# A slot table of 64-byte lines, and gathers that leave out the rows of empty slots, in an attention and mixture-of-experts kernel

## The chip, the cores and the metric

One core of one Trainium2 chip. The time is device microseconds of one launch. The kernel before was timed three times: 1839.61, 1846.12 and 1847.39 us, median 1846.12. The profile is of one execution, whose span from the first to the last instruction is 1837.7 us.

## The reference

The input `x` is 16 sequences of 1024 tokens of 512 values, float32. In short:

```
x = x + cross_attention(layernorm(x), context)      # 8 heads of 64, 64 context rows a sequence
X = layernorm(x)                                    # 16384 tokens, 512 values
scores = sigmoid(X @ gate.T)                        # 32 experts
idx    = top_k(scores + bias, 4)                    # 4 experts a token; the bias only selects
w      = scores[idx] / sum(scores[idx])
pos    = how many earlier (token, choice) pairs took the same expert
valid  = pos < 512                                  # an expert takes its first 512 pairs, no more
ye     = (silu(xe @ W1) * (xe @ W3)) @ W2           # per expert, on its 512 rows xe
out    = x + sum over choices of w * ye[expert, pos], where valid
           + silu(X @ sw1.T) * (X @ sw3.T) @ sw2.T  # shared expert, for all tokens
```

How the tokens spread over the experts depends on the drawn bias and weights. Worked out from the reference on its own inputs: of 65,536 (token, choice) pairs 6900 are valid. Thirteen experts have all 512 slots taken (1, 2, 5, 10, 14, 16, 17, 19, 20, 21, 23, 24, 28), four have 26, 87, 128 and 3 (11, 15, 22, 27), the other fifteen have none.

## The kernel before

The work has two phases. The **token phase** takes the 16384 tokens in 128 tiles of 128, in a software pipeline written out by hand: step `n` does, for tile `n - lag`, each stage with its lag (the constants `X_LOAD` = 2 to `TABLE` = 20). PE computes the attention scores (L417), the mix of values (L432, from probabilities that are turned by a DMA transpose into `pt_h` and `pt_l`), the routing logits and the shared expert (L459, L469). For a group of four tiles DVE then picks the four best experts of each token, counts with PE's help how many earlier tokens took the same expert, and writes into `slot` the number `expert * 512 + pos`, or a number past the end of the table where `pos` is over 511 (`slot_list`, L997). The normalized tokens and, in the last 32 columns, their 32 expert weights (`wfull`) are stored as rows of 544 floats in `x2aug`; the rows 16384 to 16895 of it are zero.

At the start SP stores zeros in those rows and fills the table (L347) with the numbers of the zero rows, so that an empty slot names one of them. This `fill` is made by POOL's iota and stands in `xr`, the ring of token tiles, before tokens are loaded there.

The **expert phase** takes the experts 0 to 31 in order, in a second hand-written pipeline (`GATHER`, `TURN`, `UP`, `DOWN`, `SCATTER` = 0, 1, 2, 3, 5 steps behind). SP loads the whole table into `idx` in two DMAs (L1229 and L1230), the first for experts 0 and 1. POOL gathers the expert's 512 rows in four chunks of 128 (L1245) into a ring of six buffers `rows`, PE transposes them (L1306) and multiplies (L1280, L1320), DVE scales the result by the weight that came with the row (L1426), and POOL adds it into `out` with an indirect, accumulating store (L1257). A round of four such stores waits until the round before has landed (`added`), since two experts may add to one row. Rows of empty slots are added to 512 rows behind the output proper. In POOL's queue the order of a step is the scatter of expert n - 5, then the gather of expert n.

A chunk's gather from the seventh expert on waits for `y_read` of the expert that used the buffer before.

Of the kernel before, what the change touches and what calls it, by code (L numbers as in the profile page):

```python
# [30 lines left out]
P = 128  # L31
# [12 lines left out]
ROW = D + E  # L44
PAD = CAP
EPS = 1e-5
SKIP = float(1 << 20)
# [70 lines left out]
def after(eng, sem, count):  # L118

    if count > 0:  # L120
        eng.wait_ge(sem, count)

def build(nc, x, xT, ctxT, wqT, wk, wv, wo, bo, gateT, bias, w1, w3, w2, sw1T, sw3T, sw2T, out):
    x2aug = nc.dram_tensor("x2aug", (TOKENS + PAD, ROW), F32, kind="Internal").ap()
    table = nc.dram_tensor("slot_table", (SLOTS, 1), I32, kind="Internal").ap()
    tokens_and_experts(nc, x, xT, ctxT, wqT, wk, wv, wo, bo, gateT, bias, w1, w3, w2, sw1T, sw3T, sw2T, out, x2aug, table)

def tokens_and_experts(nc, x, xT, ctxT, wqT, wk, wv, wo, bo, gateT, bias, w1, w3, w2, sw1T, sw3T, sw2T, out, x2aug, table):  # L130
    stack = ExitStack()
    with stack:
# [83 lines left out]
        ht_l = sb("ht_l", [P, KI, 4 * P], F32R)  # L216
        tok = sb("tok", [P, TILES], I32)
        slot = sb("slot", [P, 2, 4, TOP], I32)
        slot_f = sb("slot_f", [P, 4, 8], F32)
# [16 lines left out]
        zrow = xr[:, 8:10, :].rearrange("p a d -> p (a d)")[:, 0:ROW]  # L236
        fill = xr[:, 10, 0:SLOTS // P].bitcast(I32)
        down_raw = xr[:, 11, :].bitcast(BF16).rearrange("p (c d) -> p c d", c=KI)
# [63 lines left out]
        with nc.Block() as block:  # L302
            @block.sync
            def _(sp):
# [20 lines left out]
                def set_up():  # L325
# [17 lines left out]
                    for r in range(TOKENS, TOKENS + PAD, P):  # L343
                        sp.dma_start(x2aug[r:r + P, :], zrow).then_inc(fill_stored, 16)
                        sp.dma_start(out[r:r + P, :], zrow[:, 0:D]).then_inc(fill_stored, 16)
                    sp.wait_ge(fill_set, 1)
                    sp.dma_start(table.rearrange("(e p c) o -> p e (c o)", e=E, p=P),  # L347
                                 fill.rearrange("p (e c) -> p e c", e=E)).then_inc(fill_stored, 16)
# [48 lines left out]
                for n in range(STEPS):  # L397
                    step(n)
                for r in range(2):
                    sp.wait_ge(scattered[r], GROUPS // 2 * 256)  # L400
# [341 lines left out]
            def _(pool):  # L742
                def file(t, first, end):
                    if t is None:
                        return
                    g, i = t // 4, t % 4
                    if i == 0 and first == 0:
                        if g == 0:
                            pool.wait_ge(fill_stored, (2 * PAD // P + 1) * 16)
                            pool.wait_ge(const_set, 11)  # L750
                        pool.wait_ge(slots_ready, g + 1)
                        pool.sem_inc(passed, 1)
                    for q in range(first, end):
                        pool.indirect_dma_start(  # L754
                            table, bass.IndirectOffsetOnAxis(ap=slot[:, g % 2, i, q:q + 1], axis=0),
                            tok[:, t:t + 1], None, bounds_check=SLOTS - 1, oob_is_err=False).then_inc(scattered[g % 2], 16)

                def step(n):
# [17 lines left out]
                    if t is not None:  # L776
# [11 lines left out]

                pool.iota(fill.rearrange("p (e c) -> p e c", e=E), [[0, E], [1, CAP // P]], base=TOKENS,
                          channel_multiplier=CAP // P).then_inc(fill_set, 1)  # L790
# [31 lines left out]
            def _(dve):  # L822
# [164 lines left out]
                def slot_spread(g):  # L987
                    dve.wait_ge(placed, g + 1)
                    after(dve, slots_ready, g)
                    dve.sem_inc(passed, 1)  # L990
# [3 lines left out]
                def slot_list(g):  # L994
                    dve.wait_ge(spread, g * 4 + 4)
                    after(dve, scattered[g % 2], (g // 2) * 256)
                    dve.tensor_scalar(slot[:, g % 2, :, :], slot_f[:, :, 0:TOP], -1.0, TOPSLOT, ALU.mult,  # L997
                                      ALU.add).then_inc(slots_ready, 1)
# [162 lines left out]
def experts(nc, stack, ident, w1, w3, w2, out, x2aug, table):  # L1161
# [11 lines left out]
    ident_r = sb("ident_r", [P, P], F32R)  # L1173
    idx = sb("idx", [P, E, CHUNKS], I32)
    down_w = sb("down_w", [P, 2, KI, D], F32R)
    weights_rest = sb("weights_rest", [P, 3072 - 256 - 2048], F32)
    up_more = sb("up_more", [P, WEIGHT_SETS - EARLY_SETS, KD, 2 * I], BF16)
# [8 lines left out]
    he_l = sb("he_l", [P, 2, KI, CAP], F32R)  # L1186
    ye = sb("ye", [P, 4, CHUNKS, D], F32)

    TE_ps = [pb(f"TE_ps{n}") for n in range(2)]
# [17 lines left out]
    down_src = w2.rearrange("e (c p) d -> e p c d", p=P)  # L1207
    table_src = table.rearrange("(e p c) o -> p e (c o)", e=E, p=P)

# [18 lines left out]
    def experts_sync(sp):  # L1228
        sp.dma_start(idx[:, 0:2, :], table_src[:, 0:2, :]).then_inc(idx_first, 16)  # L1229
        sp.dma_start(idx[:, 2:E, :], table_src[:, 2:E, :]).then_inc(idx_loaded, 16)  # L1230
        for e in range(WEIGHT_SETS, E):
            load_weights(sp, e)

    def experts_gpsimd(pool):
        def gather(e):
# [7 lines left out]
            for c in range(CHUNKS):  # L1243
                landed = gathered[r] if e else first_rows[c]
                pool.indirect_dma_start(  # L1245
                    rows[:, r, c, :].bitcast(F32), None, x2aug,
                    bass.IndirectOffsetOnAxis(ap=idx[:, e, c:c + 1], axis=0),
                    bounds_check=TOKENS + PAD - 1, oob_is_err=False).then_inc(landed, 16)

        def scatter(e):  # L1250
# [3 lines left out]
            for c in range(CHUNKS):  # L1254
                pool.wait_ge(y_read, e * CHUNKS + c + 1)
                pool.sem_inc(passed, 1)
                pool.indirect_dma_start(  # L1257
                    out, bass.IndirectOffsetOnAxis(ap=idx[:, e, c:c + 1], axis=0),
                    ye[:, e % 4, c, :], None, bounds_check=TOKENS + PAD - 1, oob_is_err=True,
# [236 lines left out]
```

## Time and profile before

| | busy us | share of the span |
|---|---|---|
| span of the profiled execution | 1837.7 | |
| PE (matmul) | 1666.3 | 91% |
| DVE | 1384.2 | 75% |
| ACT | 1075.6 | 59% |
| POOL | 1257.2 | 68% |
| DMA queue q1 (SP's) | | 56.2% of 16 engines |
| DMA queue q0 (POOL's) | | 20.7% of 16 engines |

The profile does not list a total of its own beside the span; the three timed runs are those above. The token phase reaches to about 1358 us on PE, the expert phase from about 1385 us to the end. Busy time of an engine says how long its instructions ran, not that they were needed by the end; what stands in brackets behind a row of the timeline is how long the engine had been idle before it and what released it. "DMA share" is the mean busy share of the 16 DMA engines; it can come out over 1.

### The profile page before, as it was taken

The page shows a single profiled execution, that of the slowest core. Times are in us where ns is not written, and L with a number is a line of the kernel's source. Part 1 is how long each engine was busy: PE and PEld are TensorE (multiplying, and loading weights), DVE is VectorE, ACT ScalarE, POOL GpSimd, SP SyncE. Part 2 cuts the span into 40 slices and gives each one's busy share as a digit, 9 for nine tenths or more (in the row PEclk, how much of TensorE's full clock was granted, in tenths as well). Part 3 has the DMA queues.
Part 4 walks back from the last instruction along what each step waited for, and adds up shares of the span by engine and source line. Part 5 has one row for each costly group of instructions (what it writes and reads, how often), then busy time and mean ns, then how long its engine had stood idle before and what let it go on. Part 6 is the DMA issues. An engine that isn't in the chain of part 4 may idle for free. (4 is left out here: it accounts for less than half of the span.)

```text
span 1837.7 us, 31673 instructions
## 1 busy us (share of the span) xinstructions
PE 1666.3 (91%) x8928; PEld 1041.6 (57%) x8928; DVE 1384.2 (75%) x3450; ACT 1075.6 (59%) x2376; POOL 1257.2 (68%) x1109
## 2 busy tenths in 40 slices
PE   6896789999999999999999999999736999999993
PEld 4563455656656666666666666665423555555551
DVE  4765667888899889789879888999734777777772
ACT  4773556667777767777777767776403444444440
POOL 1333556677777777777777777777775787888774
PEclk8998899999999999999999999999877999999996
DMA  9549997787678667666756766666677999999985
GB/s 220 142 128 97 132 117 167 147 167 159 154 183 177 155 162 167 164 173 167 176 152 162 185 167 157 168 169 165 153 192 170 217 230 222 233 224 212 172 140 73
DMA packets 474482, 308.61 MB, mean 168 GB/s; under 512 B 339138, under 2 KB 381378, under 8 KB 474308
## 3 DMA queue, kind: packets, MB, share of 16 engines
q1 hardware_dynamic: 429252, 237.07, 56.2%
q0 software_dynamic: 45056, 69.52, 20.7%
q8 instruction: 73, 1.20, 0.3%
q14 instruction: 101, 0.83, 0.2%
HBM read 134.07 MB, written 105.25 MB: 130 GB/s over the span
## 5 line engine op out<-in xcount | busy, mean ns | idle before, releaser
L754 POOL DMA_INDIRECT slot_table<-tok,slot x512 | 538.0, 1051 | 140.9 <-issue 136.8
L763 POOL TENSOR_TENSOR xt_l<-xt,xt_h 128x512 fp32r<-128x512 f32 x128 | 165.4, 1292 | 191.5 <-ACT xt_h L639 191.5
L1257 POOL DMA_INDIRECT out<-ye,idx x128 | 202.9, 1585 | 70.7 <-issue 36.6
L432 PE MATMUL O_ps<-m_h,pt_h 128*128 128x512 f16 x512 | 200.2, 391 | 52.5 <-DMA pt_l<-p_l 52.0
L687 ACT ACTIVATE prob<-S_ps,rs 128x512 f32<-128x512 f32 x128 | 88.0, 687 | 244.1 <-DVE S_ps L1047 218.7
L417 PE MATMUL S_ps<-a_h,xt_h 128*128 128x512 f32 x512 | 222.4, 434 | 5.6 <-POOL xt_l L763 5.0
L778 POOL TENSOR_TENSOR prob<-prob,rsum 128x512 f32<-128x512 f32 x128 | 135.8, 1061 | 115.8 <-DVE rsum L1083 115.4
L417 PE MATMUL S_ps<-a_h,xt_l 128*128 128x512 f32 x512 | 201.3, 393 | 0.0
L417 PE MATMUL S_ps<-a_l,xt_h 128*128 128x512 f32 x512 | 201.1, 393 | 0.0
L432 PE MATMUL O_ps<-m_l,pt_h 128*128 128x512 f16 x512 | 199.1, 389 | 0.0
L432 PE MATMUL O_ps<-m_h,pt_l 128*128 128x512 f16 x512 | 198.8, 388 | 0.0
L1245 POOL DMA_INDIRECT rows<-x2aug,idx x128 | 132.8, 1037 | 43.0 <-issue 41.2
L432 PEld LDWEIGHTS O_ps<-m_h,pt_h 128*128 128x128 f16 x512 | 50.6, 99 | 138.0 <-DMA pt_l<-p_l 60.4
L1034 DVE TENSOR_TENSOR x_l<-x,x_h 128x512 f16<-128x512 f32 x128 | 91.6, 716 | 49.0 <-ACT x_h L664 48.9
L1372 ACT ACTIVATE xe_h<-TE_ps 128x512 f16<-128x512 f32 x128 | 75.7, 592 | 72.9 <-PE TE_ps L1306 72.9
L1418 DVE TENSOR_TENSOR xe_l<-TE_ps,xe_h 128x512 f16<-128x512 f32 x128 | 87.8, 687 | 40.2 <-ACT xe_h L1372 38.2
L417 PEld LDWEIGHTS S_ps<-a_h,xt_h 128*128 128x128 f32 x512 | 97.4, 190 | 35.6 <-issue 16.9
L1306 PE MATMUL TE_ps<-ident_r,rows 128*128 128x128 f32 x512 | 67.4, 257 | 49.9 <-DMA rows<-x2aug,idx 29.4
L1320 PE MATMUL YE_ps<-down_w,he_h 128*128 128x512 f32 x256 | 110.9, 433 | 0.6 <-DVE he_l L1412 0.6
L417 PEld LDWEIGHTS S_ps<-a_l,xt_h 128*128 128x128 f32 x512 | 97.2, 190 | 24.1 <-issue 7.4
L1354 ACT ACTIVATE the<-GE_ps 128x512 f32<-128x512 f32 x64 | 38.2, 597 | 121.8 <-PE GE_ps L1280 121.8
L417 PEld LDWEIGHTS S_ps<-a_h,xt_l 128*128 128x128 f32 x512 | 96.6, 189 | 21.4
(199 smaller groups left out, 4679.0 us busy)
## 6 DMA issues: line engine op xcount, KB each, us to landing
xt<-in_xT SPq DMA_DIRECT2D x128, 256.0 KB, 3.3
xr<-in_x SPq DMA_DIRECT2D x64, 512.0 KB, 4.3
x2aug<-x SPq DMA_DIRECT2D x128, 256.0 KB
out<-xr SPq DMA_DIRECT2D x64, 512.0 KB, 3.5
up_more<-in_w SPq DMA_DIRECT2D x36, 256.0 KB, 5.3
slot_table<-tok,slot POOLq DMA_INDIRECT x512
up_w<-in_w SPq DMA_DIRECT2D x28, 256.0 KB, 4.8
down_more<-in_w SPq DMA_DIRECT2D x18, 256.0 KB, 6.3
```

What stands on the lines that cost most here:

```text
L417: last = pe.matmul(S_ps[t % 2][:, :], left[:, kc, :], right[:, b % 2, kc, :], start=(m == 0), stop=(m == 3 * KD - 1))
L432: last = pe.matmul(O_ps[:, :], left[:, t % 2, p, :], right[:, b % 2, p, :], start=(m == 0), stop=(m == 3 * PAIRS - 1))
L687: act.activation(prob[:, t % 2, :, :], S_ps[t % 2][:, :].rearrange("p (h j) -> p h j", h=H), ACT.Exp, scale=rs[:, q % 2, 0, t % 2:t % 2 + ...
L754: pool.indirect_dma_start(table, bass.IndirectOffsetOnAxis(ap=slot[:, g % 2, i, q:q + 1], axis=0), tok[:, t:t + 1], None, bounds_check=SLO ...
L763: pool.tensor_tensor(xt_l[:, t % 2, :, :], xt[:, t % 2, :, :], xt_h[:, t % 2, :, :].bitcast(F32), ALU.subtract).then_inc(xt_lo, 1)
L778: pool.tensor_tensor(prob[:, t % 2, :, :], prob[:, t % 2, :, :], rsum[:, :].unsqueeze(2).to_broadcast([P, H, SKV]), ALU.mult).then_inc(pro ...
L1034: dve.tensor_tensor(x2_l[:, :], x2[:, s13 % 2, :], x2_h[:, :], ALU.subtract).then_inc(x2_lo, 1)
L1245: pool.indirect_dma_start(rows[:, r, c, :].bitcast(F32), None, x2aug, bass.IndirectOffsetOnAxis(ap=idx[:, e, c:c + 1], axis=0), bounds_che ...
L1257: pool.indirect_dma_start(out, bass.IndirectOffsetOnAxis(ap=idx[:, e, c:c + 1], axis=0), ye[:, e % 4, c, :], None, bounds_check=TOKENS + P ...
L1320: last = pe.matmul(YE_ps[i % 2][:, :], part[:, e % 2, c, i * P:(i + 1) * P], down_w[:, e % 2, c, :], start=(n == 0), stop=(n == 2 * KI - 1))
L1372: act.activation(xe_h[:, e % TURNED, :, i * P:(i + 1) * P], TE_ps[i % 2][:, :].rearrange("p (c t) -> p c t", c=KD), ACT.Copy).then_inc(t_h ...
L1418: dve.tensor_tensor(xe_l[dst], TE_ps[i % 2][:, :].rearrange("p (c t) -> p c t", c=KD), xe_h[dst], ALU.subtract).then_inc(t_lo, 1)
```

## The change

The table's slots become lines of 16 int32 (64 bytes): the fill, the filing and the index load move lines in place of single numbers, and DVE copies the token number 16 times (`tok_line`). POOL's filing waits for that copy too. SP waits for the last stores of weights ahead of the index load. From the seventh expert on (`e >= RING`, 6) the bound of the gather ends before the zero rows, so that rows of empty slots are left out and the buffer keeps what it had there; the results computed from them go, as before, to the rows behind the output. `idx` moves to the end of the expert phase's memory.

```diff
@@ -43,6 +43,7 @@
 KI = I // P
 ROW = D + E
 PAD = CAP
+LINE = 16
 EPS = 1e-5
 SKIP = float(1 << 20)
 TOPSLOT = float(1 << 22)
@@ -123,7 +124,7 @@
 
 def build(nc, x, xT, ctxT, wqT, wk, wv, wo, bo, gateT, bias, w1, w3, w2, sw1T, sw3T, sw2T, out):
     x2aug = nc.dram_tensor("x2aug", (TOKENS + PAD, ROW), F32, kind="Internal").ap()
-    table = nc.dram_tensor("slot_table", (SLOTS, 1), I32, kind="Internal").ap()
+    table = nc.dram_tensor("slot_table", (SLOTS, LINE), I32, kind="Internal").ap()
     tokens_and_experts(nc, x, xT, ctxT, wqT, wk, wv, wo, bo, gateT, bias, w1, w3, w2, sw1T, sw3T, sw2T, out, x2aug, table)
 
 
@@ -215,6 +216,7 @@
         ht_h = sb("ht_h", [P, KI, 4 * P], F32R)
         ht_l = sb("ht_l", [P, KI, 4 * P], F32R)
         tok = sb("tok", [P, TILES], I32)
+        tok_line = sb("tok_line", [P, 2, 4, LINE], I32)
         slot = sb("slot", [P, 2, 4, TOP], I32)
         slot_f = sb("slot_f", [P, 4, 8], F32)
         wfull = sb("wfull", [P, 2, 4, E], F32)
@@ -234,7 +236,7 @@
         down_ready = sem("token_down_ready")
 
         zrow = xr[:, 8:10, :].rearrange("p a d -> p (a d)")[:, 0:ROW]
-        fill = xr[:, 10, 0:SLOTS // P].bitcast(I32)
+        fill = xr[:, 16:20, :].rearrange("p a d -> p (a d)")[:, 0:SLOTS // P * LINE].bitcast(I32)
         down_raw = xr[:, 11, :].bitcast(BF16).rearrange("p (c d) -> p c d", c=KI)
         bo_raw = xr[0:33, 12, :]
         mean_q = xr[:, 13, 0:PAIRS]
@@ -344,7 +346,7 @@
                         sp.dma_start(x2aug[r:r + P, :], zrow).then_inc(fill_stored, 16)
                         sp.dma_start(out[r:r + P, :], zrow[:, 0:D]).then_inc(fill_stored, 16)
                     sp.wait_ge(fill_set, 1)
-                    sp.dma_start(table.rearrange("(e p c) o -> p e (c o)", e=E, p=P),
+                    sp.dma_start(table.rearrange("(e p c) l -> p e (c l)", e=E, p=P),
                                  fill.rearrange("p (e c) -> p e c", e=E)).then_inc(fill_stored, 16)
 
                 def step(n):
@@ -397,6 +399,8 @@
                 for n in range(STEPS):
                     step(n)
                 for r in range(2):
+                    sp.wait_ge(w_stored[r], GROUPS // 2 * 16)
+                for r in range(2):
                     sp.wait_ge(scattered[r], GROUPS // 2 * 256)
                 experts_sync(sp)
 
@@ -748,12 +752,12 @@
                         if g == 0:
                             pool.wait_ge(fill_stored, (2 * PAD // P + 1) * 16)
                             pool.wait_ge(const_set, 11)
-                        pool.wait_ge(slots_ready, g + 1)
+                        pool.wait_ge(slots_ready, 2 * g + 2)
                         pool.sem_inc(passed, 1)
                     for q in range(first, end):
                         pool.indirect_dma_start(
                             table, bass.IndirectOffsetOnAxis(ap=slot[:, g % 2, i, q:q + 1], axis=0),
-                            tok[:, t:t + 1], None, bounds_check=SLOTS - 1, oob_is_err=False).then_inc(scattered[g % 2], 16)
+                            tok_line[:, g % 2, i, :], None, bounds_check=SLOTS - 1, oob_is_err=False).then_inc(scattered[g % 2], 16)
 
                 def step(n):
                     t = at(n, XT_SPLIT)
@@ -786,7 +790,7 @@
                 pool.affine_select(out=ident[:, :], in_=ident[:, :], compare_op=ALU.not_equal, fill=1.0,
                                    base=0, pattern=[[-1, P]], channel_multiplier=1).then_inc(ident_set, 1)
 
-                pool.iota(fill.rearrange("p (e c) -> p e c", e=E), [[0, E], [1, CAP // P]], base=TOKENS,
+                pool.iota(fill.rearrange("p (e c l) -> p e c l", e=E, l=LINE), [[0, E], [1, CAP // P], [0, LINE]], base=TOKENS,
                           channel_multiplier=CAP // P).then_inc(fill_set, 1)
                 pool.memset(earlier[:, :], 0.0).then_inc(const_set, 1)
                 pool.wait_ge(const_set, 1)
@@ -986,7 +990,7 @@
 
                 def slot_spread(g):
                     dve.wait_ge(placed, g + 1)
-                    after(dve, slots_ready, g)
+                    after(dve, slots_ready, 2 * g)
                     dve.sem_inc(passed, 1)
                     for i in range(4):
                         dve.max(slot_f[:, i, :], over[:, i, :]).then_inc(spread, 1)
@@ -994,6 +998,7 @@
                 def slot_list(g):
                     dve.wait_ge(spread, g * 4 + 4)
                     after(dve, scattered[g % 2], (g // 2) * 256)
+                    dve.tensor_copy(tok_line[:, g % 2], tok[:, 4 * g:4 * g + 4].unsqueeze(2).to_broadcast([P, 4, LINE])).then_inc(slots_ready, 1)
                     dve.tensor_scalar(slot[:, g % 2, :, :], slot_f[:, :, 0:TOP], -1.0, TOPSLOT, ALU.mult,
                                       ALU.add).then_inc(slots_ready, 1)
 
@@ -1171,9 +1176,8 @@
     up_w = sb("up_w", [P, 4, KD, 2 * I], BF16)
     down_raw = sb("down_raw", [P, 4, KI, D], BF16)
     ident_r = sb("ident_r", [P, P], F32R)
-    idx = sb("idx", [P, E, CHUNKS], I32)
     down_w = sb("down_w", [P, 2, KI, D], F32R)
-    weights_rest = sb("weights_rest", [P, 3072 - 256 - 2048], F32)
+    weights_rest = sb("weights_rest", [P, 3072 - 128 - 2048], F32)
     up_more = sb("up_more", [P, WEIGHT_SETS - EARLY_SETS, KD, 2 * I], BF16)
     down_more = sb("down_more", [P, WEIGHT_SETS - EARLY_SETS, KI, D], BF16)
     rows = sb("rows", [P, RING, CHUNKS, ROW], F32R)
@@ -1185,6 +1189,7 @@
     he_h = sb("he_h", [P, 2, KI, CAP], F32R)
     he_l = sb("he_l", [P, 2, KI, CAP], F32R)
     ye = sb("ye", [P, 4, CHUNKS, D], F32)
+    idx = sb("idx", [P, E, CHUNKS, LINE], I32)
 
     TE_ps = [pb(f"TE_ps{n}") for n in range(2)]
     GE_ps = [pb(f"GE_ps{n}") for n in range(KI)]
@@ -1205,7 +1210,7 @@
 
     up_src = [w.rearrange("e (c p) i -> e p c i", p=P) for w in (w1, w3)]
     down_src = w2.rearrange("e (c p) d -> e p c d", p=P)
-    table_src = table.rearrange("(e p c) o -> p e (c o)", e=E, p=P)
+    table_src = table.rearrange("(e p c) l -> p e c l", e=E, p=P)
 
     def up_set(e):
         r = e % WEIGHT_SETS
@@ -1226,8 +1231,8 @@
         sp.dma_start(down_set(e), down_src[e]).then_inc(set_loaded[r], 16)
 
     def experts_sync(sp):
-        sp.dma_start(idx[:, 0:2, :], table_src[:, 0:2, :]).then_inc(idx_first, 16)
-        sp.dma_start(idx[:, 2:E, :], table_src[:, 2:E, :]).then_inc(idx_loaded, 16)
+        sp.dma_start(idx[:, 0:2, :, :], table_src[:, 0:2, :, :]).then_inc(idx_first, 16)
+        sp.dma_start(idx[:, 2:E, :, :], table_src[:, 2:E, :, :]).then_inc(idx_loaded, 16)
         for e in range(WEIGHT_SETS, E):
             load_weights(sp, e)
 
@@ -1244,8 +1249,9 @@
                 landed = gathered[r] if e else first_rows[c]
                 pool.indirect_dma_start(
                     rows[:, r, c, :].bitcast(F32), None, x2aug,
-                    bass.IndirectOffsetOnAxis(ap=idx[:, e, c:c + 1], axis=0),
-                    bounds_check=TOKENS + PAD - 1, oob_is_err=False).then_inc(landed, 16)
+                    bass.IndirectOffsetOnAxis(ap=idx[:, e, c, 0:1], axis=0),
+                    bounds_check=(TOKENS if e >= RING else TOKENS + PAD) - 1,
+                    oob_is_err=False).then_inc(landed, 16)
 
         def scatter(e):
             if e:
@@ -1255,7 +1261,7 @@
                 pool.wait_ge(y_read, e * CHUNKS + c + 1)
                 pool.sem_inc(passed, 1)
                 pool.indirect_dma_start(
-                    out, bass.IndirectOffsetOnAxis(ap=idx[:, e, c:c + 1], axis=0),
+                    out, bass.IndirectOffsetOnAxis(ap=idx[:, e, c, 0:1], axis=0),
                     ye[:, e % 4, c, :], None, bounds_check=TOKENS + PAD - 1, oob_is_err=True,
                     compute_op=ALU.add).then_inc(added, 16)
```

## Rows read from the trace of the kernel before

**Rows 1.** Stretches: window, length, busy time by engine, clock, DMA share, GB/s.
```profile
100.00:136.00 36.00, 35.02 (x212) 23.53 (x211) 28.32 (x79) 26.00 (x62) 10.81 (x10) 1.00 0.55 140
...
136.00:276.00 140.00, 104.76 (x510) 61.11 (x508) 85.53 (x243) 69.60 (x163) 70.04 (x66) 0.89 1.04 115
...
276.00:420.00 144.00, 138.50 (x761) 87.53 (x761) 117.82 (x319) 98.89 (x229) 101.45 (x93) 0.99 0.79 156
...
730.00:886.00 156.00, 156.00 (x867) 99.26 (x866) 134.78 (x373) 112.23 (x262) 116.50 (x105) 1.00 0.67 168
```

**Rows 2.** Waits, 136 to 276 us: total, times, longest.
```profile
PE O_ps L432 <- DMA pt_l<-p_l: 33.8, 8, 12.7
```

**Rows 3.** DMA issues, 137 to 277 us: count, size, median to landing.
```profile
xt<-in_xT SPq DMA_DIRECT2D x10, 256.0 KB, 7.4
...
x2aug<-wfull SPq DMA_DIRECT2D x3, 64.0 KB, 7.4
```

**Rows 4.** DMA issues, 800 to 940 us.
```profile
xt<-in_xT SPq DMA_DIRECT2D x14, 256.0 KB, 3.5
...
x2aug<-wfull SPq DMA_DIRECT2D x3, 64.0 KB, 3.2
```

**Rows 5.** POOL over time: start, duration; first filings of tiles, two others.
```profile
137.14 1.17 POOL L754 DMA_INDIRECT slot_table<-tok,slot  x1 [0.17 <-issue]
...
139.93 0.98 POOL L754 DMA_INDIRECT slot_table<-tok,slot  x1 [0.30 <-issue]
...
276.63 1.00 POOL L754 DMA_INDIRECT slot_table<-tok,slot  x1 [0.16 <-issue]
...
419.78 1.00 POOL L754 DMA_INDIRECT slot_table<-tok,slot  x1 [0.17 <-issue]
...
731.26 1.00 POOL L754 DMA_INDIRECT slot_table<-tok,slot  x1 [0.17 <-issue]
...
1040.95 1.00 POOL L754 DMA_INDIRECT slot_table<-tok,slot  x1 [0.17 <-issue]
...
1375.90 0.98 POOL L754 DMA_INDIRECT slot_table<-tok,slot  x1 [0.30 <-issue]
```

**Rows 6.** The start: landing of the fill, then POOL and ACT over time.
```profile
slot_table<-xr SPq DMA_DIRECT2D x1, 64.0 KB, 13.8
...
3.71 0.48 POOL L789 IOTA xr<- 128x128 int32 x1
...
38.68 0.63 ACT L639 ACTIVATE xt_h<-xt 128x512 fp32r<-128x512 f32 x1 [6.23 <-DMA xt<-in_xT]
```

**Rows 7.** Start of the expert phase: index load and its landing, POOL, PE.
```profile
1378.49 0.46 SPq L1230 DMA_DIRECT2D idx<-slot_table  x1
...
idx<-slot_table SPq DMA_DIRECT2D x1, 60.0 KB, 4.5
...
1381.15 1.04 POOL L1245 DMA_INDIRECT rows<-x2aug,idx  x1 [4.27 <-issue]
...
1384.65 0.59 PE L1306 MATMUL TE_ps<-ident_r,rows 128*128 128x128 f32 x3 [27.19 <-DMA rows<-x2aug,idx]
```

**Rows 8.** Chain that ended last: two experts' first products.
```profile
1759.82 1.74 PE GE_ps L1280 x8
...
1772.61 1.74 PE GE_ps L1280 x8
```

**Rows 9.** POOL over time, late in the expert phase.
```profile
1744.79 1.62 POOL L1257 DMA_INDIRECT out<-ye,idx  x1 [0.53 <-issue]
...
1752.33 1.08 POOL L1245 DMA_INDIRECT rows<-x2aug,idx  x1 [0.30 <-issue]
...
1765.17 1.08 POOL L1245 DMA_INDIRECT rows<-x2aug,idx  x1 [0.30 <-issue]
...
1782.74 1.55 POOL L1257 DMA_INDIRECT out<-ye,idx  x1 [5.01 <-DMA out<-ye,idx]
```

**Rows 10.** Instructions that write `slot`: ns min/median/max.
```profile
L997 DVE TENSOR_SCALAR slot<-slot_f x32: 239/942/1299, 126.0 to 1349.0; 128x16 int32<-128x16 f32 x32
```

## The prediction

> **What bounds the kernel now.** I read busy time by stretch first, then the waits and DMA landings of the stretches that looked bad, then POOL in order of time.
>
> The token phase has two regimes. From 730 to 886 us PE is busy 156.00 of 156 us at full clock, and the DMA engines are 0.67 occupied while moving 168 GB/s. From 136 to 276 us PE is busy only 104.76 of 140 us, its granted clock is 0.89, and the DMA engines are occupied 1.04 while moving just 115 GB/s: more engine time, fewer bytes. From 276 to 420 it is nearly over (138.50 of 144 us). Just before, from 100 to 136 us, there is nothing wrong (35.02 of 36 us, DMA 0.55) [rows 1]. In the bad stretch PE's lost time is a wait for the transposed low half of the probabilities, 33.8 us in 8 waits [rows 2]. That transfer is not alone in being late: a 256 KB load of `xt` takes 7.4 us to land there and 3.5 us at 800 to 940 us, the 64 KB store of `wfull` 7.4 us against 3.2 [rows 3, 4].
>
> What begins at 137 us is the filing of tokens into the slot table [rows 5]: four indirect stores a tile, 4 bytes for each (token, choice). What fades out by 420 us is the number of those that write: a slot past an expert's 512th is out of bounds and left out. Routing worked out from the reference on its own inputs gives 512 real writes in each of tiles 0 to 4, then 442, 410, 356, 333, 275, about 112 a tile in tiles 10 to 23, 977 in all the 104 tiles after: 6900 of 65,536. So the stall follows the count of 4-byte writes, and neither the instructions (512 of them, evenly spread) nor the bytes. Consecutive tokens of one expert fill consecutive 4-byte slots, so tile 0's 512 writes lie in 37 lines of 64 bytes, some 14 writes to a line, from many DMA engines at once.
>
> In steady state a tile takes (1040.95 - 731.26) / 32 = 9.68 us. Tiles 0 to 9 took 276.63 - 137.14 = 139.5 us, against 96.8; tiles 10 to 23 took 143.2 against 135.5 [rows 5]. The excess is 42.7 + 7.7 = **50.4 us**.
>
> In the expert phase PE takes 1772.61 - 1759.82 = 12.79 us an expert [rows 8] and POOL 1765.17 - 1752.33 = 12.84 us, four adding scatters and four gathers back to back [rows 9]. POOL's chain sets the end: each round of scatters waits for the round before to land, and in the last four rounds that costs about 5 us each (5.01) with gathers long over [rows 9].
>
> **The change, part by part.** The sum is made against the profiled execution's span, 1837.7 us; the three timed runs (1839.61 to 1847.39, median 1846.12) lie 1.9 to 9.7 above, and I add 8.4, the median's.
>
> *Table writes of 64 bytes.* Each written slot now covers a line of its own and no two writes share one. The upper bound of the gain is the 50.4 us; the lower is nothing or a loss. Nearest rows: the `wfull` store is 512 pieces of 128 bytes, issued once in four tiles, and the phase stays smooth with it (3.2 us to land) [rows 4]; that speaks for full recovery. The filling of the table at the start writes 4096 pieces of 16 bytes, four to a 64-byte line, and takes 13.8 us for 64 KB [rows 6], far worse than 64 KB of `wfull`. If its extra (13.8 - 3.2 = 10.6 us for 4096) were the cost of any piece under a line's size or at it, the 5923 writes of tiles 0 to 23 would keep 15 us. I keep a third, 5 us, since the 128-byte row is the nearer in size and full in its lines. **-45 us.** PE is what is late next: in the good stretch it has no idle at all, so a tile can't go under about 9.7 us.
>
> *POOL's issues.* Same count. A store whose 128 rows were all written took 0.98 us (139.93 us) and one with none also 0.98 (1375.90) [rows 5]; the gather of 2176-byte rows at 1381.15 took 1.04 [rows 7]. At 0.02 us more each, only those behind PE's last token work count, some 20: +0.4 us, taken as **+0.5**.
>
> *DVE's copy* into `tok_line` (128x64, int32), 32 times. The nearest is `slot` at the same place: 239 ns at best, 942 median, 1299 at worst [rows 10]; 8 to 42 us of DVE in all. DVE is busy 134.78 of 156 us in steady state [rows 1], about 1.3 us free a tile, 5 a group, against 1 us of copy a group; PE hides it, at worst the copy is exposed each time (+30). I take **+1**. POOL's filing is released one DVE instruction later; behind it in POOL's queue stand the next product with `rsum` and the next split of `xt`. The copy waits for the landing of the stores of two groups back, as `slot` did.
>
> *Fill.* POOL's iota grows 16-fold. Now 0.48 us, at 3.71 us [rows 6]; even at 16 times, 7.7 us, POOL's set-up would end before 14 us, and POOL has nothing more to do until ACT has split the first `xt` tile: nothing. The store becomes 4096 pieces of 256 bytes, 1 MB. Queued behind it is the `xt` load that ACT waited 6.23 us for, until 38.68 us [rows 6]. By size, 1 MB is four `xt` loads of 3.5 us [rows 4], 14 us, no gain; at the 168 GB/s of the smooth stretch [rows 1] it is 6.2 us. It is issued some 14 us before 38.68, about 2 us of pad stores stand ahead of it, and 6.2 more put its landing near 33 us: **-4.5**, between -6 and +1.
>
> *SP's new wait* for `w_stored` stands ahead of the index load, with the later weight loads behind. The last of these stores is issued in step 145; the last filing belongs to step 147, and POOL issues it at 1375.90 with PE's token work long over [rows 5, 7]. Nothing. *Index load:* 1 MB in place of 64 KB. The second part is issued at 1378.49, and the first gather, at 1381.15, feeds PE's first transpose at 1384.65 after 27.19 us idle [rows 7]; it lands in 4.5 us now. With 1 MB it shares the engines with the first gathers. Nothing at best; at worst the 1 MB at 168 GB/s, 6.2 us, less the 2.7 between issue and gather, goes ahead of them: 3.5. **+1.** Everything after, POOL's chain too, moves with it.
>
> *Gathers that leave rows out.* Of the 13,312 rows of experts 6 to 31, 5364 are filled, so 7948 (17 MB) go. PE never waits for a gather after the first four, so the bytes buy nothing directly. POOL issues as many instructions, and by the two 0.98 us rows a left-out row is no cheaper to issue. What it frees is the scatters' landing: eight times between 1445 and 1770 us POOL waited 0.35 to 0.62 us instead of 0.30 before a round (0.53 at 1744.79 [rows 9]), 1.9 us over. **-2.** The last rounds have no gathers beside them and stay.
>
> Sum: -45 + 0.5 + 1 - 4.5 + 1 - 2 = -49; span 1789, time **1797 us**.
>
> The Trainium skill has a rule that speaks against this change ("DMA: Bandwidth & Descriptors", Specifications): transfers under 512 B make the DMA engine read, modify and write. 64 bytes are as far under as 4 are, and by it the -45 goes. The trace doesn't bear the rule out at 128 bytes, where 512 pieces land in 3.2 us; at 4 and 16 bytes it agrees. It is rival B.
>
> **The rivals.**
>
> A. Half cure: real writes of a line still stall, with the 16-byte fill's price rather than `wfull`'s. 15 to 30 us of the 50 stay: 1807 to 1822. For it: the number of real writes is unchanged, 2048 a group against 512 for `wfull`. Against: no stall with `wfull`.
>
> B. No cure: the stall is per small write, whatever its size. Then 0.5 + 1 - 4.5 + 1 - 2 = -4, 1842; without the fill's gain 1847. For it: the stall follows the count of writes. Against: `wfull` again, and that 4096 16-byte writes cost some 11 us while 5923 of 4 bytes cost 50, 8.5 ns against 2.6 a piece: the price rose with the writes to one line.
>
> C. Slower: the memory pays per line opened. Today tile 0 opens 37 lines, after the change 512. If neighbours are merged today and the 50 us are the price of lines, more lines cost more; at twice, +50, 1892. It decides against the change as soon as the line-wise price outgrows 50 + 4 us. For it: nothing directly. Against: the fill's 64 KB opens 1024 lines for 11 us, tiles 0 to 4 some 230 lines for over 20.
>
> D. The leaving out does more than I give it: POOL's issue shrinks when few rows remain. POOL runs about 10 us behind PE's results at the end, so at most 10 us more: 1787. Against: the two 0.98 us rows. That it does nothing at all costs me 2 us.
>
> **How the numbers follow.** My forecast (1785 to 1807, D's gain within it) 0.65; A 0.16; B 0.11; C 0.08. The range, 1783 to 1829, takes in the forecast and A and leaves out B and C. 0.5% is 9 us, what a measurement of this kernel can tell from no change: all of the forecast and A are faster (0.81), with 0.02 of B; the rest of B is the same (0.09); C is slower (0.08).
>
> **What would show it.** Right: from 136 to 276 us PE busy over 130 us at clock 0.98 or more and DMA occupied near 0.7; PE's wait for the transposed probabilities under 5 us there; tile 10's first filing some 40 us sooner after tile 0's; the fill landing under 10 us; the first transpose within 8 us of the last filing; POOL's round still 12.8 us and gathers still 1.04 us; the waits over 0.30 before scatters gone. Wrong: a DMA share near 1 in that stretch (A, B), a tile period over 14 us (C), or a steady tile above 9.8 us, which would be DVE's copy.

## The result: 1781.1 us, 3.4% faster

The changed kernel took 1781.11 us in the median of four runs (1776.43 to 1785.63), the kernel before, with one more run beside it, 1842.86 (1834.57 to 1847.39). The ratio is 0.9656, with a 95% interval of 0.9614 to 0.9699. In a later comparison on one chip it was 1778.98 us (six runs) against 1845.02 (seventeen), ratio 0.9645 (0.9614 to 0.9677). Forecast were 1797 us and a range from 1783: right in direction and in its main mechanism, too small in size, and the range begins 2 us too high.

The profiled execution of the changed kernel spans 1779.9 us, 57.8 less than before. Its stretch from 25 to 40 us and two of the stretches of [rows 1] (window, length, busy time of PE, PEld, DVE, ACT and POOL, clock, DMA share, GB/s):

```profile
25.00:40.00 15.00, 12.00 (x35) 6.71 (x35) 7.33 (x27) 11.59 (x32) 3.60 (x3) 0.89 0.70 194
136.00:276.00 140.00, 140.00 (x766) 87.64 (x765) 123.97 (x350) 102.54 (x242) 105.12 (x95) 1.00 0.75 176
276.00:420.00 144.00, 144.00 (x798) 92.11 (x797) 124.58 (x347) 103.11 (x242) 106.08 (x97) 1.00 0.69 168
```

The bad stretch is gone altogether. PE is busy in all 140 us where it was busy in 104.76, does 766 matmuls instead of 510, and has its full clock; the DMA engines move 176 GB/s in place of 115 with three quarters of their time. Among the waits of 136 to 276 us PE's on the turned probabilities (33.8 us, [rows 2]) no longer appears. An `xt` load is one of 15 in the same 140 us, not of 10, and `wfull` lands in 3.0 us in place of 7.4 [rows 3]:

```profile
xt<-in_xT SPq DMA_DIRECT2D x15, 256.0 KB
x2aug<-wfull SPq DMA_DIRECT2D x4, 64.0 KB, 3.0
```

POOL over time, the first filings of tiles 0, 10 and 24 and the last one of all (start, duration), against [rows 5]:

```profile
131.96 1.17 POOL L758 DMA_INDIRECT slot_table<-tok_line,slot  x1 [0.19 <-issue]
...
226.45 1.50 POOL L758 DMA_INDIRECT slot_table<-tok_line,slot  x1 [0.15 <-issue]
...
361.81 1.00 POOL L758 DMA_INDIRECT slot_table<-tok_line,slot  x1 [0.17 <-issue]
...
1314.48 0.97 POOL L758 DMA_INDIRECT slot_table<-tok_line,slot  x1 [0.30 <-issue]
```

Tiles 0 to 9 take 226.45 - 131.96 = 94.5 us where they took 139.5, tiles 10 to 23 135.4 where they took 143.2. The other lines follow from such starts. The kernel's time, stretch by stretch:

| stretch | before | after | difference | forecast |
|---|---|---|---|---|
| start to the first filing | 137.1 | 132.0 | -5.2 | -4.5 |
| tiles 0 to 9 | 139.5 | 94.5 | -45.0 | |
| tiles 10 to 23 | 143.2 | 135.4 | -7.8 | |
| tiles 24 to the last filing | 956.1 | 952.7 | -3.4 | |
| the three lines above | | | -56.2 | -43.5 |
| last filing to the first transpose | 8.8 | 9.9 | +1.2 | +1 |
| from there to the sixth expert's gather | 40.8 | 37.3 | -3.5 | 0 |
| 26 rounds of POOL | 339.7 | 344.7 | +5.0 | -2 |
| last gathers to the end | 72.5 | 73.5 | +1.0 | 0 |

Two of these lines can be followed further in the traces. Of the -3.4, 1.8 us lie in tiles 24 to 111 and most of the rest in tiles 112 to 119, a stretch that differs by up to 4.5 us between the kernels below. And the +5.0 of the 26 rounds is waiting: the time by which POOL's idle before the first adding store of a round exceeds the usual 0.30 us adds up to 8.0 us in 14 of the 26 rounds, where it was 2.5 us in 9 before. Of the five longest the profile puts three (1.0 to 1.5 us) down to the landing of the round before and two to DVE's `ye`. The longest:

```profile
1607.28 1.62 POOL L1263 DMA_INDIRECT out<-ye,idx  x1 [1.94 <-DVE ye L1432]
```

The two ends of the start and of the expert phase, to be held against [rows 6] and [rows 7]: the fill's landing, POOL's iota, ACT's second split, the index load with its landing, the first gather and the first transpose.

```profile
slot_table<-xr SPq DMA_DIRECT2D x1, 1024.0 KB, 7.5
...
3.71 2.34 POOL L793 IOTA xr<- 128x2048 int32 x1
...
33.17 0.63 ACT L643 ACTIVATE xt_h<-xt 128x512 fp32r<-128x512 f32 x1 [0.66 <-DMA xt<-in_xT]
...
1317.11 0.46 SPq L1235 DMA_DIRECT2D idx<-slot_table  x1
...
idx<-slot_table SPq DMA_DIRECT2D x1, 960.0 KB, 6.4
...
1320.04 1.04 POOL L1250 DMA_INDIRECT rows<-x2aug,idx  x1 [4.58 <-issue]
...
1324.42 1.33 PE L1312 MATMUL TE_ps<-ident_r,rows 128*128 128x128 f32 x8 [27.75 <-DMA rows<-x2aug,idx]
```

Sixteen times the bytes land in 7.5 us instead of 13.8, in as many pieces (4096, of 256 bytes instead of 16), and ACT gets the second `xt` tile 5.5 us sooner (33.17 against 38.68). While the fill was landing, the kernel before showed the same signs as while it filed tokens, a high DMA share with few bytes:

```profile
25.00:40.00 15.00, 10.21 (x21) 4.35 (x21) 4.00 (x17) 7.54 (x23) 1.88 (x2) 0.73 1.13 113
```

### The profile page after: what moved, and what is told of

Its sections match the earlier page's. It is cut to its first block and busy times, and to the rows that moved or that the text cites. A ratio compares the mean times of both kernels' runs of the same rounds, so it can differ in the third digit from the quotient of the medians.

```text
span 1779.9 us, 31706 instructions
## 1 busy us (share of the span) xinstructions
PE 1649.4 (93%) x8928; PEld 1038.4 (58%) x8928; DVE 1387.6 (78%) x3482; ACT 1074.6 (60%) x2376; POOL 1261.9 (71%) x1109
## 5 line engine op out<-in xcount | busy, mean ns | idle before, releaser
L758 POOL DMA_INDIRECT slot_table<-tok_line,slot x512 | 541.0, 1057 | 141.1 <-issue 137.2
L436 PE MATMUL O_ps<-m_h,pt_h 128*128 128x512 f16 x512 | 196.1, 383 | 8.4 <-DMA pt_l<-p_l 8.4
L436 PE MATMUL O_ps<-m_l,pt_h 128*128 128x512 f16 x512 | 194.9, 381 | 0.0
L436 PE MATMUL O_ps<-m_h,pt_l 128*128 128x512 f16 x512 | 194.8, 380 | 0.0
L1432 DVE TENSOR_SCALAR ye<-YE_ps,rows 128x512 f32<-128x512 f32 x128 | 95.2, 744 | 10.9 <-PE YE_ps L1326 8.3
```

Source lines behind the costliest of these rows:

```text
L436: last = pe.matmul(O_ps[:, :], left[:, t % 2, p, :], right[:, b % 2, p, :], start=(m == 0), stop=(m == 3 * PAIRS - 1))
L758: pool.indirect_dma_start(table, bass.IndirectOffsetOnAxis(ap=slot[:, g % 2, i, q:q + 1], axis=0), tok_line[:, g % 2, i, :], None, bounds_ ...
L1432: dve.tensor_scalar(ye[:, e % 4, i, :], YE_ps[i % 2][:, :], w, None, ALU.mult).then_inc(y_read, 1)
```

## The experiments

**Which part of the change did it.** The lines without the leaving out, the leaving out without the lines, and the change again, five rounds each on one chip. Beside them ran one more step, told further down: the adding stores leave out empty slots too.

Lines alone:
```diff
-                    bounds_check=(TOKENS if e >= RING else TOKENS + PAD) - 1,
+                    bounds_check=TOKENS + PAD - 1,
```

> The change without its gathers: every gather takes all 512 rows of its expert, the zero rows too. Theory: the 64-byte lines give the whole gain and the leaving out gives nothing, so 1781 us (1777 to 1786), the first ten tiles of the filing take 94 to 97 us, and the span's loss against the forecast sits in POOL's rounds. In the profile of the changed kernel 26 rounds of the expert phase took 339.7 - wait for wait 13.26 us a round from gather 5 to gather 31, against 13.07 before. If the leaving out is what lengthened the rounds (rival), this kernel has 13.07 again and is about 5 us faster than the changed one; if it had won the 2 us of my forecast, it is 2 us slower.

Leaving out alone (in the kernel before):
```diff
-                    bounds_check=TOKENS + PAD - 1, oob_is_err=False).then_inc(landed, 16)
+                    bounds_check=(TOKENS if e >= RING else TOKENS + PAD) - 1, oob_is_err=False).then_inc(landed, 16)
```

> The kernel before with the change's bound on the gathers from the seventh expert on, and the 4-byte table kept. Theory: the gathers are off the path, so 1843 us, within 4 us of the kernel before; tiles 0 to 9 take 139 us as before. Rival (leaving out lengthens POOL's rounds): 1848, rounds of 13.26 us. Rival (my forecast's -2): 1841, rounds of about 13.0 us with no waits over 0.30 us.

The change again, as it stands:

> The changed kernel unchanged, beside the others on the same chip. Theory: 1781 us, tiles 0 to 9 in 94.5 us. If its POOL rounds are 13.26 us again the lengthening belongs to the kernel; if they are near 13.07 it was that one execution.

The lines alone took 1785.81 us (ratio 0.9682, 0.9651 to 0.9714): 59 of the 66 us. The leaving out alone took 1839.37 against 1845.02 (0.9981, 0.9955 to 1.0008), not to be told from nothing by itself, and its bad stretch is as before: tiles 0 to 9 took 141.1 us. The change again took 1778.98, 6.8 us under the lines alone by medians, 5.3 by means with an error of about 4. Since that is more than the 2 us of my forecast I ran the lines alone again:

> 64-byte lines alone a second time, since the leaving out's share (1785.8 against 1779.0 us, single executions spread over 8 us) was larger than the 2 us of my forecast but not by more than its error. Theory: 1784 to 1787 us again, so 4 to 7 us for the leaving out. Rival: 1781 us, and the share is my 2 us.

1786.10 us (1775.75 to 1790.51), the same again. By medians the leaving out is worth 4 to 7 us. By the means of all twelve executions of the lines alone and all ten of the change (1784.0 and 1780.0, on several chips) it is 4.1 us with a 95% interval of about 3.7 to either side, so my 2 us are not excluded. Where it is saved no profile shows.

The 26 rounds of POOL took 344.7 and 343.4 us in the two profiled executions of the change and 339.6 and 337.3 in the two of the lines alone, the other way round. By the test of the expectation the lengthening would belong to the change (343.4 / 26 = 13.21 us a round). But the kernel with 4-byte writes 64 bytes apart, below, has the changed kernel's gathers and adding stores and took 336.1 us, and the four other kernels that leave out the gathers' empty rows alone took 336.1 to 337.4. So the leaving out doesn't lengthen the rounds by itself. The rounds are longer where POOL waits longer before an adding store: the excess of these waits was 8.0 and 6.9 us in the two executions of the change, 4.4 and 2.1 with the lines alone, and 0.5 to 2.1 in those five. Why it differs so between executions is open. The profiled executions of the lines alone were the second fastest and the fastest of their six (1780.9 and 1775.8 us), the change's in the later comparison its slowest (1783.2), so the profiles can't be set against each other as if they were medians.

**Size of a write, or writes that meet.** Three kernels with other tables, all with the leaving out. First: 4-byte writes, each in a 64-byte line of its own. The table stays at 1 MB, fill, index load and DVE's copy stay as in the change; the two lines that matter:

```diff
-                            tok_line[:, g % 2, i, :], None, bounds_check=SLOTS - 1, oob_is_err=False)
+                            tok[:, t:t + 1], None, bounds_check=SLOTS * LINE - 1, oob_is_err=False)
...
-                    dve.tensor_scalar(slot[:, g % 2, :, :], slot_f[:, :, 0:TOP], -1.0, TOPSLOT, ALU.mult,
+                    dve.tensor_scalar(slot[:, g % 2, :, :], slot_f[:, :, 0:TOP], -float(LINE), TOPSLOT * LINE, ALU.mult,
```

> The changed kernel, but each filing writes 4 bytes, the first word of its slot's own 64-byte line (the place is 16 times the slot). Fill and index load as in the change. Tells the size of a write from the sharing of a line. Theory (the stall is several writes meeting in one 64-byte line): tiles 0 to 9 take 94 to 98 us as in the changed kernel, 1781 us. Rival (a write of less than a line stalls, shared or not): 135 to 140 us, and some 1832 us.

It took 1775.06 us (two runs; ratio 0.9609, 0.9531 to 0.9686), and its stretch from 136 to 276 us is the changed kernel's:

```profile
136.00:276.00 140.00, 140.00 (x766) 87.61 (x765) 123.98 (x350) 102.61 (x242) 105.22 (x95) 1.00 0.74 174
```

The writes are as small and as many as in the kernel before, and nothing stalls. So it was not the size. Then lines of 16 and of 32 bytes:

```diff
-LINE = 16
+LINE = 4        # the other kernel: 8
```

> The changed kernel with lines of 4 int32: 16-byte writes, four slots to 64 bytes, and the fill in pieces of 64 bytes. Theory (sharing): the excess of tiles 0 to 9 falls with the writes to a line, by the price of the 16-byte fill 2.6 ns x 4946 writes = 10 to 15 us of the 43, tiles 0 to 9 in 104 to 112 us, 1791 to 1797 us. Rival (any write under a line): 135 to 140 us.

> The changed kernel with lines of 8 int32: 32-byte writes, two slots to 64 bytes. Theory (sharing of 64-byte lines): a small rest, tiles 0 to 9 in 96 to 103 us, 1783 to 1788 us. Rival (the unit is 32 bytes, not 64): no rest at all, 94.5 us. Rival (any write under 64 bytes): 135 to 140 us.

16 bytes took 1785.72 us, 32 bytes 1777.27 (two runs each). For 16 bytes the first filings of tiles 0 and 10 are:

```profile
132.74 1.17 POOL L758 DMA_INDIRECT slot_table<-tok_line,slot  x1 [0.19 <-issue]
...
231.38 1.50 POOL L758 DMA_INDIRECT slot_table<-tok_line,slot  x1 [0.15 <-issue]
```

and its stretch from 136 to 276 us:

```profile
136.00:276.00 140.00, 137.53 (x738) 84.59 (x738) 120.55 (x338) 98.38 (x231) 101.34 (x92) 0.99 0.79 168
```

Tiles 0 to 9: 139.5 us with sixteen slots to 64 bytes, 98.6 with four, 94.6 with two, 94.5 with one. The price falls much faster than the number of slots that share a line. What is left at four is 4.1 us there, less than the expected 10 to 15. (Tiles 0 to 9 hold 4376 real writes; the 4946 of the expectation is a slip.) This kernel also loses 4.6 us in tiles 24 to 119, but 4.5 of them in tiles 112 to 119, where few tokens are filed and where the kernel with 4-byte writes 32 bytes apart (below), which has no stall in its first ten tiles, loses 2.5 us as well. That part is not shown to be the table's.

At 32 bytes the expectation missed: 96 to 103 us for tiles 0 to 9 and 1783 to 1788 us in all if the unit that writes must not share is 64 bytes, and 94.5 us if it is 32. Measured were 94.6 us and 1777.27 us, the rival's figures. The runs so far fit a unit of 32 bytes without more, and one of 64 only if two slots to a line cost nothing.

**A small table, or a crowded line.** With 64-byte lines the table is also sixteen times as large. To tell that apart the 64 KB table was kept and its slots dealt out, neighbours 64 bytes apart (the copy on DVE is gone, fill and index load follow the new order in pieces of 256 bytes, and the gathers' empty rows are left out):

```diff
-                    dve.tensor_scalar(slot[:, g % 2, :, :], slot_f[:, :, 0:TOP], -1.0, TOPSLOT, ALU.mult, ALU.add)
+                    dve.tensor_scalar(slot_raw[:, :, :], slot_f[:, :, 0:TOP], -1.0, TOPSLOT, ALU.mult, ALU.add)
+                    dve.tensor_scalar(slot_line[:, :, :], slot_raw[:, :, :], 1023, 4, ALU.bitwise_and, ALU.logical_shift_left)
+                    dve.scalar_tensor_tensor(slot[:, g % 2, :, :], slot_raw[:, :, :], 10, slot_line[:, :, :],
+                                             ALU.logical_shift_right, ALU.bitwise_or)
```

> A 64 KB table of 4-byte slots as before, but dealt out: slot s stands at word (s mod 1024) * 16 + s / 1024, so consecutive slots lie 64 bytes apart and the 16 words of a line belong to slots 1024 apart. The leaving-out gathers are in; no lines, no DVE copy, two more small DVE operations a group, and the fill and the index load are 256 pieces of 256 bytes (64 KB each). Tells writes that meet in a line at the same time from the size or the spread of the table. Theory (meeting in a line): tiles 0 to 9 in 94 to 98 us, 1774 to 1781 us, the first transpose about 1 us sooner than with the 1 MB load. Rival (a small table is a crowded table: few banks or channels for 64 KB): 120 to 140 us for these tiles and 1810 us or more.

```profile
136.00:276.00 140.00, 140.00 (x766) 87.43 (x765) 121.42 (x351) 102.14 (x240) 104.17 (x95) 1.00 0.72 175
```

1782.67 us (0.9663, 0.9635 to 0.9692), tiles 0 to 9 in 94.5 us, with the old 4-byte writes in the old 64 KB. The rival that a small table is a crowded one has fallen too. What stalls is several writes at nearby addresses within a short time: neighbours 4 bytes apart stall, 16 bytes apart a little, 32 and 64 bytes apart not at all. Worked out from the reference's routing, one indirect store in tiles 0 to 9 puts on average 5.0 writes into each 64-byte line that it touches in the kernel before, 2.0 with slots of 16 bytes, 1.4 with 32, 1.1 in the dealt table and 1.0 with 64; the stall was 45.0, 4.1, 0.1, 0 and 0 us. In units of 32 bytes the averages are 3.2, 1.4, 1.0, 1.04 and 1.0. Both rows fit.

The time missed its 1774 to 1781 us by under 2. The first transpose came 3.6 us after the first gather; in the seven profiled executions with a 1 MB index load it came 4.4 to 5.1 us after, in the seven with a smaller one 3.5 to 3.6, so that load costs about a microsecond. Tiles 24 to 119 took 914.7 us against 910.8, spread evenly over them; the cause was not looked for.

**The end of the kernel.** The forecast's other claim was that POOL's chain sets the end, through the landing of the adding stores.

```diff
-                    ye[:, e % 4, c, :], None, bounds_check=TOKENS + PAD - 1, oob_is_err=True,
+                    ye[:, e % 4, c, :], None, bounds_check=TOKENS - 1, oob_is_err=False,
```

> The changed kernel, and the adding stores leave out empty slots as well (bound 16384 in place of 16896). 9484 of 16,384 added rows go. Theory: POOL's chain sets the end and its length hangs on the landing of each round. With experts 29, 30 and 31 empty, the wait ahead of the last rounds falls from 5.0 to 5.5 us to about 1.3 (as the table's last, empty filing shows), and the landing after the last round too: about 3 x 3.8 = 11 us; the waits within the rounds of the steady stretch go as well, some 5 to 10 us down to PE's 12.79 us an expert. In all 10 to 20 us: 1761 to 1771 us. Rival: the end hangs on PE and on the number of instructions alone, and an empty store costs a full receipt: 1779 to 1783.

1764.71 us (1762.65 to 1765.73; ratio 0.9569, 0.9539 to 0.9598), 14.3 under the change beside it. POOL at the starts of the last four rounds, and the last row of all:

```profile
1716.67 1.54 POOL L1263 DMA_INDIRECT out<-ye,idx  x1 [2.12 <-DMA out<-ye,idx]
...
1729.26 1.54 POOL L1263 DMA_INDIRECT out<-ye,idx  x1 [5.28 <-DMA out<-ye,idx]
...
1738.88 1.54 POOL L1263 DMA_INDIRECT out<-ye,idx  x1 [2.13 <-DMA out<-ye,idx]
...
1748.07 1.54 POOL L1263 DMA_INDIRECT out<-ye,idx  x1 [2.13 <-DVE ye L1432]
...
1753.61 1.54 POOL L1263 DMA_INDIRECT out<-ye,idx  x1 [0.30 <-issue]
```

After the round of expert 28, which is full, POOL waits 5.28 us; after those of 27 (three rows), 29 and 30 it waits 2.12 to 2.13, not 1.3 as expected. The excess of the waits within the 26 rounds is 1.9 us, and the rounds take 336.9 us. From the last gathers to the end it is 61.7 us instead of 73.5. Do the gathers' rows matter beside that?

```diff
-                    bounds_check=(TOKENS if e >= RING else TOKENS + PAD) - 1,
+                    bounds_check=TOKENS + PAD - 1,
...
-                    ye[:, e % 4, c, :], None, bounds_check=TOKENS + PAD - 1, oob_is_err=True,
+                    ye[:, e % 4, c, :], None, bounds_check=TOKENS - 1, oob_is_err=False,
```

> 64-byte lines, every gather takes all its rows, but the adding stores leave out empty slots. Tells how the gathers' rows cost time. Theory: they cost it only through the landing of the adding stores, which POOL waits for; with 9484 of 16,384 added rows gone those land early whatever the gathers move, so this kernel is within 2 us of the one that leaves out both (1764.7), and 26 rounds take 335 to 338 us. Rival: gathered rows cost POOL or PE time directly; then the 5 us between the lines alone and the changed kernel stay, 1770 us.

1764.92 us (0.9586, 0.9565 to 0.9607), and 26 rounds in 336.2 us: as with both left out, to the few us that two comparisons on different chips can tell. So no cost of the gathered rows' own is seen; with the empty adds gone, nothing is seen that leaving them out would win. That fits the account that they cost time by making adds land later; it doesn't show the landing itself.

**Combinations.** The dealt table with the adds left out, and 4-byte writes 32 bytes apart (`LINE = 8`, no `tok_line`) with the adds left out:

> The dealt table, and the adding stores leave out empty slots as well. If both hold: the 14 us that leaving out adds won on the 64-byte table, on top of the dealt kernel: 1758 to 1766 us. Rival: the dealt table stalls and this is over 1790.

> 4-byte writes 32 bytes apart (two slots to a 64-byte line), no copy on DVE, 512 KB of fill and index load, adds of empty slots left out too. By the 32-byte and the four-bytes-apart kernels there is no stall left: tiles 0 to 9 in 94.5 us, 1758 to 1764 us. If the DVE copy had cost anything in the changed kernel, tiles 24 to 119 fall under 910.8 us here; theory: they stay within 1 us.

1766.83 us (0.9572, 0.9544 to 0.9600) and 1764.61 (0.9562, 0.9536 to 0.9589), each under 1 us above its expected range. All versions that leave out the adds lie between 1764.6 and 1766.8 us, 12 to 17 us under the changed kernel, and no table is seen to be better than another. With 4-byte writes 32 bytes apart tiles 0 to 9 took 94.6 us, so at this distance too it isn't the size of the write that cures. Without the DVE copy tiles 24 to 119 took 913.3 us, not fewer than 910.8 and not within 1 us of it; 2.55 of the 2.6 us more lie in tiles 112 to 119. No cost of the copy is seen.

## Why the prediction was wrong in size

*The stall is due to the small writes, and lines cure it.* Right, and by more than was said; that no two writes share a line, the reason that I gave, is what counts, and their smallness is not. The step that failed is "I keep a third, 5 us": the price of the 16-byte fill was carried over to 64-byte lines. With writes of 16 bytes 4.1 us of the 45.0 in tiles 0 to 9 are left, a third of what that price gives for them; at 32 and 64 bytes none is left. Two smaller parts of the same term: without the stall tiles 0 to 9 run at 9.45 us and not at the 9.68 of the later ones (2.3 us). PE is busy throughout there, with 51.1 matmuls to a tile where tiles 10 to 23 have 54.3, so the upper bound of 50.4 us was no bound. And the excess was ended at tile 24, where the stretch behind it came out 3.4 us shorter. At most 1.8 us of that, in tiles 24 to 111, can be the 977 late writes; whether they are is open. The term measured 56.2 us with DVE and POOL in it, against 43.5.

*DVE's copy +1, POOL's issues +0.5.* Nothing is seen of either: POOL's stores into the table took 1.055 us on average after and 1.052 before. The copy and the place calculation behind it (ns min/median/max), to be held against [rows 10]:

```profile
L1001 DVE COPY tok_line<-tok x32: 194/962/1300, 120.8 to 1287.8; 128x64 int32<-128x64 int32 x32
...
L1002 DVE TENSOR_SCALAR slot<-slot_f x32: 159/160/1285, 121.7 to 1287.9; 128x16 int32<-128x16 f32 x32
```

The median 0.94 us of `slot` seems not to be that instruction's own work: the copy, now first there, shows it, and `slot` behind the copy takes 0.16. So the real addition is some 0.2 us a group.

*The fill -4.5, the index load +1.* Measured -5.2 and +1.2. The sign "first transpose within 8 us of the last filing" was set wrong: it was 8.8 us in the kernel before and 9.9 after.

*The leaving out -2.* 4 to 7 us by medians, 4.1 by means with 2 not excluded; where it is saved is open. The mechanism that I gave was not seen in the profiled execution: the waits over 0.30 us before scatters, which were to go, grew from 2.5 to 8.0 us, and the rounds with them, +5.0 where the term said -2. In the kernel before with the leaving out alone they were 0.5 us, so the mechanism isn't refuted either. That a left-out row is no cheaper for POOL to issue held: gathers took 1.047 us on average after, 1.037 before.

*Adding 8.4 us for what lies around the span.* Wrong, and larger than any single part of the table's miss. In every execution on record the time is over its own span by 1.8 us for the changed kernel (1779.9 and 1781.71; 1781.4 and 1783.16) and by 2.1 to 2.2 for the kernel before. The span of 1837.7 thus belongs to an execution of about 1840 us, a fast one; the median was above it because executions of the kernel before spread from 1833.2 to 1855.2. Those of the changed kernel spread from 1775.2 to 1785.6. With 1.8 in place of 8.4 the forecast would have been 1790.5, and with the table's term at its upper bound about 1785. The distance of a median from one profiled execution was carried over as a constant; by medians the change won 62 and 66 us, by the two profiled executions 57.8.

So the miss of 16 us is 12.7 from the table's term, 6.6 from this one, 0.7 from the start and 3.5 from a stretch before the sixth gather that I had at 0, less 7.0 of the rounds and about 1 at the end; the rest is small terms and the 0.6 us by which the profiled execution lies above the median. The last three came from no reason of mine, and that they partly cancelled is luck.

*The rivals.* A (half cure) is what happens at 16 bytes, and weaker; B and C fell: 512 lines opened a tile cost nothing. The rule of the Trainium skill that I set against the change ("DMA: Bandwidth & Descriptors", Specifications: read, modify, write below 512 B) gives no time here: 4-byte writes in lines of their own don't stall. No run here shows whether such a write is a read, a change and a write; the price was in writes that met. D is not seen in POOL's issue times.

*What was left out.* The rounds' +5.0, the -3.5 before the sixth gather and the +1.0 at the end came without any edit of mine to explain them. From the first gather to the sixth expert's there are two values, 41.3 to 42.6 or 44.2 to 44.7 us, in fourteen profiled executions; the change and the lines alone show one of each, so it is the execution's.

## What to carry to other kernels

Where DMA engines are busy and move little, look for what is written, not for how much: count the writes that fall within 32 or 64 bytes at about the same time, by working out the indices if need be. Spreading neighbours apart is enough, 32 bytes in this kernel; neither larger writes nor a larger table are needed. In a chain of accumulating stores that wait for one another, leave out the empty rows of the stores first; those of the loads won about 4 us here, and nothing that could be seen once the stores were quick. And before adding a kernel's median to its profile's span, see which execution the profile is of.

## What was not expected of the hardware

Some 5900 writes of 4 bytes (24 KB of 309 MB moved) cost this kernel over 50 us, nearly all of it in other transfers: their own queue was occupied 2.0% in the bad stretch, and an `xt` load beside them took twice its time. The dependence is steep: sixteen, four, two and one slot to a line of 64 bytes left 45, 4, 0 and 0 us over in the first ten tiles. Whether the unit is 64 bytes or 32 these runs don't tell. A round of adding stores with no or three rows to write still takes 2.1 us until the next can start, against 5.0 to 5.5 for a full one.
